# Linear attention layer: output normalisation in four 512-token blocks per head instead of in each 128-token chunk

## The reference, cut to what matters

```python
# per sequence t=2048, H=8 heads of width 128, CHUNK=128
def step(S, qkv):
    qb, kb, vb = qkv
    attn = where(causal, qb @ kb.T, 0)
    o = attn @ vb + qb @ S
    S = S + kb.T @ vb
    return (S, o)
o = rmsnorm(o, out_norm_w)     # o * rsqrt(mean(o*o over the head's 128) + eps) * w
return o @ Wo                  # after the heads are put side by side
```

## Time and profile before

| | us |
|---|---|
| median of 3 runs | 28465.1 (28440.7 to 28501.19) |
| the profiled execution | 28485.89 |
| its span on the slowest core (core 3) | 28484.4 |
| spans of the 8 cores | 28418.2 to 28484.4 |

### The profile page before, as it was taken

One profiled execution on the slowest core, in us unless ns is written; L12 is line 12 of the kernel. 1 busy time (PEld: TensorE's weight loads), 2 busy tenths in 40 slices (PEclk: granted clock), 3 DMA queues, 4 the chain that ended last, 5 costly groups with the idle time before them and its releaser, 6 DMA issues.

```text
span 28484.4 us, 160669 instructions; the slowest of 8 cores (28418.2 to 28484.4 us)
## 1 busy us (share of the span) xinstructions
PE 10588.0 (37%) x36548; PEld 4113.5 (14%) x36548; DVE 7100.5 (25%) x17733; ACT 4097.4 (14%) x7775; POOL 1706.6 (6%) x2214
## 2 busy tenths in 40 slices
PE   3444434334322222124443444444444322223444
PEld 1111101101011111011111111111111111111211
DVE  1200132232233333331112100223223233333211
ACT  1100121121111111000011000212112111111000
POOL 0000010110100000000000000011011000000000
PEclk6677655555555555556766767555555555555677
DMA  1044311211211111323330244221121111110233
GB/s 28 13 52 52 52 16 18 21 16 18 23 22 26 23 26 25 121 70 122 122 94 10 32 52 52 36 21 15 19 21 15 22 25 26 24 25 19 88 120 117
DMA packets 2238689, 1206.69 MB, mean 42 GB/s; under 512 B 1805384, under 2 KB 2104528, under 8 KB 2227536
## 3 DMA queue, kind: packets, MB, share of 16 engines
q0 software_dynamic: 1324848, 799.82, 17.2%
q1 hardware_dynamic: 912928, 396.59, 5.8%
HBM read 1333.09 MB, written 41.96 MB: 48 GB/s over the span
## 4 chain that ended last, share of the span: by engine, by line
PE 34%; DMA 22%; DVE 19%; issue 13%; ACT 7%; POOL 2%; DVEq 1%; SPq 1%; ACTq 0%; POOLq 0%; PEldq 0%
DMA WBUF<-f_w2cat 6%; PE pb L922 4%; DMA WBUF<-scr_wq 3%; DMA WBUF<-f_refine_w 3%; DMA WBUF<-l_wup 3%; DVE CSTAT L1290 3%; PE pb L607 2%; PE pb L1607 2%; DMA WBUF<-l_wdown 2%; PE pb L638 2%; PE pb L619 2%; PE pb L1390 2%; PE pb L1282 2%; PE pb L1683 2%; PE pb L1622 2%
## 5 line engine op out<-in xcount | busy, mean ns | idle before, releaser
L922 PE MATMUL pb<-SB,WBUF 128*128 128x512 bf16 x3840 | 1675.0, 586 | 2962.5 <-DMA WBUF<-f_w2cat 2645.6
L1282 PE MATMUL pb<-WBUF 64*128 64x512 bf16 (+3 forms) x1280 | 543.7, 546 | 2837.5 <-DVE CSTAT L1342 1993.5
L1313 ACT ACTIVATE SMALL<-pb,CSTAT 128x512 bf16<-128x512 f32 (+3 forms) x1152 | 709.9, 616 | 4620.7 <-DVE CSTAT L1300 4557.5
L1390 PE MATMUL pb<-SB,WBUF 128*64 128x128 bf16 x4352 | 555.8, 310 | 2128.7 <-DVE CSTAT L1342 1855.7
L607 PE MATMUL pb<-BIGA,WBUF 128*128 128x512 bf16 x2048 | 704.3, 506 | 1360.6 <-DMA WBUF<-l_wup 1174.8
L1607 PE MATMUL pb<-WBUF,BIGA 128*128 128x512 bf16 x2048 | 694.3, 500 | 1168.1 <-DMA WBUF<-scr_wq 876.4
L1290 DVE TENSOR_REDUCE CSTAT<-pb 128x1 f32<-128x512 f32 (+3 forms) x1280 | 782.7, 611 | 955.3 <-PE pb L1282 874.6
L922 PEld LDWEIGHTS pb<-SB,WBUF 128*128 128x128 bf16 x3840 | 399.4, 122 | 3885.8 <-issue 3855.1
L638 PE MATMUL pb<-BIGB,WBUF 128*128 128x512 bf16 x2048 | 615.4, 474 | 688.3 <-DMA WBUF<-l_wdown 688.3
L1683 PE MATMUL pb<-WBUF,STREAM 128*128 128x512 bf16 x2048 | 519.8, 418 | 902.5 <-DMA STREAM<-STREAM 563.3
L931 POOL DMA_DIRECT2D WBUF<-f_w2cat x640 | 483.6, 756 | 5608.7 <-PE pb L924 5457.1
(11 more groups left out here) (286 smaller groups left out, 16685.9 us busy)
## 6 DMA issues: line engine op xcount, KB each, us to landing
WBUF<-scr_wq POOLq DMA_DIRECT2D x256, 1024.0 KB, 8.1
WBUF<-scr_wq POOLq DMA_DIRECT2D x64, 2048.0 KB, 13.2
WBUF<-f_w2cat POOLq DMA_DIRECT2D x640, 128.0 KB, 3.3
WBUF<-l_wgate POOLq DMA_DIRECT2D x128, 512.0 KB, 5.7
WBUF<-l_wup POOLq DMA_DIRECT2D x128, 512.0 KB, 7.5
WBUF<-l_wdown POOLq DMA_DIRECT2D x64, 1024.0 KB, 9.8
WBUF<-f_refine_w POOLq DMA_DIRECT2D x128, 256.0 KB, 4.3
WBUF<-f_refine_w POOLq DMA_DIRECT2D x64, 512.0 KB, 6.5
```

Of the source, the lines that this page charges most:

```text
L922: last = e.matmul(bank[:, :], Wg[:, slab + 128 * c:slab + 128 * c + 128], B["hm"](r, c), start=(c == 0), stop=False)
L1282: e.matmul(bank[:, 0:wspan], qhf[hofs:hofs + 64, 128 * qi:128 * qi + 128], khf[hofs:hofs + 64, w0:w0 + wspan], start=True, stop=True, tile ...
L1313: e.activation(pbuf[:, w0:w0 + full], bank[:, 0:full], AF.Exp, scale=0.125, bias=CS[:, 16 * h2 + 9:16 * h2 + 10], accum_out=CS[:, 16 * h2 ...
L1390: last = e.matmul(obank[0:64, 0:128], qkv[:, 2, pr2, c, 64 * h2:64 * h2 + 64], ptre[:, 128 * c:128 * c + 128], start=(c == 0), stop=(c == ...
```

## The change

In the chunk loop, the eight operations of the normalisation are gone; what is left in their place is one ACT copy of the chunk's output from `pb[4]` to `BB` as bf16, and PE's wait at the end of the body is now for ACT. After the 16 chunks of a head, a new loop of four blocks of 512 tokens normalises `BB` in place: square from `BB`, ones matmul, scale and eps, Ln, Exp, spreading matmul, and one product that reads the spread row straight from PSUM. There is no copy of the spread row to SBUF any more. Each block waits for the whole block before it.

```diff
-                kb.op("act", lambda e: e.activation(osq, pb[4][:, 0:128], AF.Square),
+                kb.op("act", lambda e, h=h, cs=cs: e.copy(BB[:, h, cs], pb[4][:, 0:128]),
                       waits=[(S["pe"], o_done)], inc=S["act"])
-                ... ones matmul, scale+eps, Ln, Exp, spreading matmul, copy, product, all 128 wide
-                kb.op("pe", lambda e: None, waits=[(S["dve"], S["dve"].val)], inc=S["pe"])
+                kb.op("pe", lambda e: None, waits=[(S["act"], S["act"].val)], inc=S["pe"])
+            row_f = SM[0:1, 1024:1536]
+            for nb4 in range(4):
+                bsl = slice(512 * nb4, 512 * nb4 + 512)
+                sqb = TIb[:, 512 * (nb4 % 2):512 * (nb4 % 2) + 512]
+                kb.op("act", lambda e, h=h, bsl=bsl, sqb=sqb: e.activation(
+                    sqb, BB[:, h, bsl], AF.Square),
+                    waits=[(S["dve"], S["dve"].val), (S["pe"], S["pe"].val)], inc=S["act"])
+                kb.op("pe", lambda e, sqb=sqb: e.matmul(pb[5][0:1, 0:512], sb["ones_b"][:, 0:1],
+                                                        sqb, start=True, stop=True),
+                      waits=[(S["act"], S["act"].val)], inc=S["pe"])
+                kb.op("dve", lambda e: e.tensor_scalar(row_f, pb[5][0:1, 0:512], 1.0 / P, EPS,
+                                                       ALU.mult, ALU.add),
+                      waits=[(S["pe"], S["pe"].val)], inc=S["dve"])
+                kb.op("act", lambda e: e.activation(row_f, row_f, AF.Ln),
+                      waits=[(S["dve"], S["dve"].val)], inc=S["act"])
+                kb.op("act", lambda e: e.activation(row_f, row_f, AF.Exp, scale=-0.5),
+                      inc=S["act"])
+                kb.op("pe", lambda e: e.matmul(pb[5][:, 0:512], sb["ones_f"][0:1, :], row_f,
                                                start=True, stop=True),
                       waits=[(S["act"], S["act"].val)], inc=S["pe"])
+                kb.op("dve", lambda e, h=h, bsl=bsl: e.scalar_tensor_tensor(
+                    BB[:, h, bsl], pb[5][:, 0:512], sb["l0_out_norm_w"][:, 0:1], BB[:, h, bsl],
                     ALU.mult, ALU.mult),
+                    waits=[(S["pe"], S["pe"].val)], inc=S["dve"])
+            kb.op("pe", lambda e: None, waits=[(S["dve"], S["dve"].val)], inc=S["pe"])
```

More of the change, by code:

```diff
@@ L536, in phase_A @@
                 kb.op("dve", lambda e: e.tensor_copy(S_sb, S_f32), inc=S["dve"])
-                kb.op("act", lambda e: e.activation(osq, pb[4][:, 0:128], AF.Square),
+                kb.op("act", lambda e, h=h, cs=cs: e.copy(BB[:, h, cs], pb[4][:, 0:128]),
                       waits=[(S["pe"], o_done)], inc=S["act"])
-                kb.op("pe", lambda e: e.matmul(pb[5][0:1, 0:128], sb["ones_b"][:, 0:1], osq,
+                kb.op("pe", lambda e: None, waits=[(S["act"], S["act"].val)], inc=S["pe"])
@@ L540, in phase_A @@
                                                start=True, stop=True),
                       waits=[(S["act"], S["act"].val)], inc=S["pe"])
[L542 to L553, removed]
@@ L554, in phase_A @@
-                rep_done = S["dve"].val
-                kb.op("dve", lambda e, h=h, cs=cs: e.scalar_tensor_tensor(
-                    BB[:, h, cs], pb[4][:, 0:128], sb["l0_out_norm_w"][:, 0:1], rep_f,
+                kb.op("dve", lambda e, h=h, bsl=bsl: e.scalar_tensor_tensor(
+                    BB[:, h, bsl], pb[5][:, 0:512], sb["l0_out_norm_w"][:, 0:1], BB[:, h, bsl],
                     ALU.mult, ALU.mult),
-                    waits=[(S["dve"], rep_done)], inc=S["dve"])
-                kb.op("pe", lambda e: None, waits=[(S["dve"], S["dve"].val)], inc=S["pe"])
+                    waits=[(S["pe"], S["pe"].val)], inc=S["dve"])
```

## The result

The changed kernel takes 27,973.0 us (median of 8 runs, 27,947.6 to 27,990.7) against 28,467.3 (8 runs, 28,440.7 to 28,501.2). The ratio is 0.9826, 95% interval 0.9815 to 0.9837: 494 us less, where 485 and a time of 27,980 were forecast. The profiled execution took 27,970.0 us, its slowest core (core 7) 27,968.5.

What follows compares the result with a forecast made beforehand. No engine total bound it; each head's chunk loop was a serial relay. A head takes 32.3 + 27.6 = 59.9 us instead of 90.2; 16 heads give 485 us, from 28,465.1 to 27,980 us, range 27,895 to 28,075.

Steps and rivals of the forecast that it cites:

- The chunk loop: Attention's loop over chunks: period falls from 5.63 to 2.01 us, made of 1.51 + 0.28 + 0.22, bounds 1.92 and 2.09.
- the 0.2 us named: Chunk loop: PE's path still ends last, by 0.2 us, so DVE's state update stays hidden.
- The loop up to the first block: A head's 16 chunks until the block loop starts: 1.90, fourteen at 2.01, then 2.30, together 32.3 us.
- The blocks: Four new normalisation blocks after a head's chunks, a serial relay: 6.94 us each, ±0.3, together 27.6 us a head.
- product and handover to ACT's next square: Last step of a block: 0.74 us for the product plus 0.15 until ACT's next square, 0.89 together.
- The head: One head's chunk loop and blocks: 59.9 us instead of 90.2, 30.3 less, 485 us in 16 heads.
- ±27 in its range: Projections: one group more or less at the slow level (4.45 against 2.76 us) in each head.
- The clock did not rise in the loop: Rival: granted clock rises in the chunk loop, 54 us less in all, total 27,926; chance 0.11.
- stay low in the projections: Rival: after sparse blocks all 12 projection groups could cost 4.45 us, 256 us lost, total 28,236; chance 0.04.
- no table load at the new lines: Forecast counted none; rival: two ACT table loads of 1.28 us in each of 64 blocks, 164 us, 28,144; chance 0.03.
- the price that the prediction quotes for a switch: ACT table switch in the blocks: about 2.66 us by the Trainium skill, an estimate of 340 us here.
- The blocks do grow with their width: Rival: blocks don't scale with width, 18 us each, 226 us more than before, total 28,690; chance 0.01.

Runs made afterwards that it cites:

- e3: Changed kernel with the chunk's output alternating between two PSUM banks, the copy wait on the output matmul instead of PE's empty wait: 27,963.5 us, 0.9830 of the kernel before.
- e5: As e3, but the wait for the copy of two chunks ago stands on the scores matmul: 27,924.8 us, 0.9814 of the kernel before.
- e1: Changed kernel without its block loop, output left unnormalised: 27,537.6 us, 0.9677 of the kernel before.
- e2: Changed kernel with 16 blocks of 128 tokens per head instead of 4 of 512: 28,442.6 us, 0.9999 of the kernel before.
- e6: Changed kernel with e5's chunk loop and e4's blocks together: 27,741.5 us, 0.9745 of the kernel before.
- e7: As e6, with a head's normalisation between the next head's projection groups, which wait only for ACT's preceding copy: 27,498.1 us, 0.9657 of the kernel before.
- e4: Changed kernel with a head's four blocks taken step by step side by side, one Ln and Exp over 2048: 27,770.8 us, 0.9765 of the kernel before.

## Why the prediction was right

**The chunk loop.** Predicted 2.01 us, measured 1.98 in most chunks. The copy took its lower bound (266 ns instead of 278), and the handover from ACT through PE's empty wait is 164.33 − 164.12 = 0.21, as taken from DVE's. DVE's update stayed hidden with the 0.2 us named; e3 and e5 show that it is what ends last once PE is freed, at 1.81 us. The loop up to the first block took 192.83 − 160.47 = 32.36 us, where 32.3 were predicted. That it came so close is in part luck: the 0.03 us saved in each of 13 chunks were taken back by the one of 2.35, which no term of the sum stood for.

**The blocks.** Predicted 6.94 us, measured 7.03. Every step came within 0.01 us of its term except the last, product and handover to ACT's next square: 0.95 against 0.89. There the wait of ACT's square for DVE and PE together takes 199.86 − 199.65 = 0.21 instead of 0.15, and in the block after it 206.89 − 206.69 = 0.20. e1 confirms their price in the time, within its interval.

**The head.** 59.9 predicted, 60.27 measured in the first: 0.31 of the excess is the blocks' (27.91 against 27.6) and 0.06 the loop's. The prediction took 90.23 us of the first head before for all 16, but their mean is 90.42. By the means a head gives 30.13 us instead of 30.3, and 16 heads 482 where 485 were counted.

**What was not counted.** The projections gained 13 us from the clock over both sequences, on the mean of the cores, which together with the heads makes the 494. The prediction carried this as ±27 in its range, without a sign. It happened to make up for what the heads fell short: luck in the size of the last few microseconds, not in the mechanism.

**The rivals.** The clock did not rise in the loop, nor did it stay low in the projections. There is no table load at the new lines: on core 7 none stands between 80.3 and 1129.7 us, where the first sequence's heads lie, and Exp starts 0.09 us after Ln. The Trainium skill (ScalarE: Activation LUTs, "Table sets: the hidden batching unit") asks that activations be batched by set; there was no load here that batching could have saved. Where this kernel does load between two activations (48 times at L955 before the change) the load stands 0.08 us behind the one and 0.01 before the other, 1.37 us in all, about half of the price that the prediction quotes for a switch. The blocks do grow with their width, if far less than in proportion, and this is exactly the gain.

## What to carry to other kernels

Where the timeline shows a relay, count the steps and the fixed part of each; taking the relay out of a loop gains nothing unless it is made wider, overlapped or put beside other work, which gave 494, 181 and 243 us here. Price such a relay from rows of the same shapes, with the gap between each pair of engines as a term of its own. A wait that is always met should stand on an instruction with time to spare.

## What the runs showed of the hardware that I had not expected

A second semaphore wait on a matmul, met long before, delayed it by 0.11 us (0.55 against 0.43 and 0.44 from the mask's start, e3 and e5). On ACT there is a hint of the same and no proof: a square that waits for DVE and PE starts 0.21 us after DVE's end, an Ln that waits for DVE 0.14, but these are two different operations.

The fast clock of the projections comes a group sooner or later from head to head and from core to core. Cores that run the same kernel in the same execution differ (0 to 14 slow spacings out of 88 in e5, some 24 us in a sequence's stage). But the means of the 8 cores differ between kernels too, in one profiled execution of each: 2 to 3 in e5, 4 to 6 in the changed kernel, e2, e6 and e7, some 8 in e1, e3 and e4, and 7 to 8 before. So the projections cannot be taken as unchanged when the loop ahead of them is changed; here that was worth 13 us in all, and 21 between e3 and e5. What sets it is left open.
